# Batch loops written out, stack loads behind a stored-maxima wait, and VectorE taking ScalarE's copies at the end of the attention

## The reference

```python
mod = (silu(c) @ wmod).reshape(8, 6, 1, 128)          # sa, ca, ga, sb, cb, gb per batch
h = layernorm(x) * (1 + ca) + sa
q, k, v = split(h @ w_qkv)                            # 16 heads of 8
x = x + ga * (softmax(q k^T / sqrt(128)) v) @ w_out
h = layernorm(x) * (1 + cb) + sb
scores = softmax(h @ w_router)                        # top 2 of 8, renormalised
x = x + gb * sum_e comb[e] * ((silu(h w_gate[e]) * (h w_up[e])) @ w_down[e])
```

## Time and profile before

| what | value |
|---|---|
| device time, median of 3 runs | 664.18 us (663.45 to 664.81) |
| profiled execution, its own device time | 666.58 us |
| its span, first to last instruction | 664.8 us |
| mean granted TensorE clock | 0.96 |
| busy: PE, DVE, ACT, POOL | 609.4, 545.0, 443.4, 267.2 us |
| attention, first exponential of batch 1 to that of batch 2 | 49.30 us |

### The profile page before, as it was taken

One profiled execution on the slowest core, in us unless ns is written; L12 is line 12 of the kernel. 1 busy time (PEld: TensorE's weight loads), 2 busy tenths in 40 slices (PEclk: granted clock), 3 DMA queues, 4 the chain that ended last, 5 costly groups with the idle time before them and its releaser, 6 DMA issues.

```text
span 664.8 us, 12806 instructions
## 1 busy us (share of the span) xinstructions
PE 609.4 (92%) x3349; PEld 282.7 (43%) x3349; DVE 545.0 (82%) x1033; ACT 443.4 (67%) x843; POOL 267.2 (40%) x384
## 2 busy tenths in 40 slices
PE   4299999999999999999999999898899999999995
PEld 3112223322322322322322322226677777777773
DVE  3698889999998999998999999417788888888884
ACT  1207878878878778878778878875465555555552
POOL 4422012222222222222222212434576786786763
PEclk9757999999999999999999999979899999999997
DMA  7712604404304304304304301154244445344401
GB/s 187 178 56 61 210 4 97 131 19 97 131 20 97 129 18 97 130 19 97 129 18 97 130 19 47 50 156 142 80 129 157 129 136 149 126 142 142 133 26 32
DMA packets 49084, 65.58 MB, mean 99 GB/s; under 512 B 9544, under 2 KB 30544, under 8 KB 49040
## 3 DMA queue, kind: packets, MB, share of 16 engines
q1 hardware_dynamic: 46416, 64.32, 33.3%
q10 hardware_dynamic: 2624, 0.79, 0.5%
HBM read 47.26 MB, written 17.83 MB: 98 GB/s over the span
## 4 chain that ended last, share of the span: by engine, by line
PE 44%; issue 17%; POOL 16%; DVE 12%; ACT 6%; DMA 2%; SPq 1%; ACTq 1%; DVEq 1%; POOLq 0%
PE o_acc L1169 15%; POOL hid_lo L601 14%; PE s_row L1142 12%; PE s_col L1155 7%; DVE negmax L853 7%; ACT probs L645 4%; DVE probs L1032 2%; PE misc L1107 1%; POOL h_lo L607 1%; PE misc L1093 1%; PE misc L1090 1%; SPq L308 1%; PE misc L1123 1%; ACT oT L649 1%; PE misc L1119 1%
## 5 line engine op out<-in xcount | busy, mean ns | idle before, releaser
L853 DVE TENSOR_REDUCE negmax<-s_row 128x1 f32<-128x512 f32 x512 | 321.6, 682 | 37.9 <-PE s_row L1142 37.1
L645 ACT ACTIVATE probs<-s_col 128x512 f32<-128x512 f32 x512 | 273.6, 599 | 75.0 <-PE s_col L1155 72.0
L1142 PE MATMUL s_row<-k_stack,q_stack 64*128 64x512 bf16 x512 | 142.4, 403 | 23.8 <-DMA k_stack<-k_scr 11.0
L601 POOL TENSOR_TENSOR hid_lo<-probs,hid_hi 128x512 fp32r<-128x512 f32 x87 | 128.5, 1493 | 61.3 <-ACT hid_hi L789 61.3
L1169 PE MATMUL o_acc<-probs,v_aug 128*32 128x512 f32 x1024 | 138.1, 612 | 0.0
L1155 PE MATMUL s_col<-q_stack,k_stack 64*128 64x512 bf16 x512 | 132.3, 384 | 6.1 <-ACT probs L645 5.1
L789 ACT ACTIVATE hid_hi<-probs 128x512 fp32r<-128x512 f32 x88 | 55.6, 632 | 86.3 <-DVE probs L1032 86.0
L1142 PEld LDWEIGHTS s_row<-k_stack,q_stack 64*128 64x128 bf16 x512 | 36.0, 93 | 177.7 <-DVE negmax L853 138.5
L1032 DVE TENSOR_TENSOR probs<-probs,q_stack 128x512 f32<-128x512 f32 x56 | 62.3, 1112 | 15.6 <-POOL hid_lo L601 13.5
L509 POOL CAST negmax_parts<-negmax 128x16 bf16<-128x16 f32 x32 | 6.3, 196 | 166.9 <-DVE negmax L853 166.9
L1022 DVE TENSOR_TENSOR probs<-probs,s_col 128x512 f32<-128x512 f32 x88 | 59.6, 677 | 3.0 <-ACT probs L809 1.6
(11 more groups left out here) (134 smaller groups left out, 684.6 us busy)
## 6 DMA issues: line engine op xcount, KB each, us to landing
q_scr<-q_parts SPq DMA_DIRECT2D x48, 128.0 KB, 2.4
k_scr<-k_parts SPq DMA_DIRECT2D x48, 128.0 KB, 2.4
q_stack<-q_scr SPq DMA_DIRECT2D x8, 768.0 KB, 6.0
k_stack<-k_scr SPq DMA_DIRECT2D x8, 768.0 KB, 7.4
q_stack<-combT_scr SPq DMA_DIRECT2D x24, 256.0 KB, 3.3
k_stack<-combT_scr SPq DMA_DIRECT2D x16, 224.0 KB, 2.8
q_stack<-combT_scr SPq DMA_DIRECT2D x16, 192.0 KB, 2.8
q_stack<-combT_scr SPq DMA_DIRECT2D x16, 160.0 KB, 2.5
```

Of the source, the lines that this page charges most:

```text
L601: nc.gpsimd.tensor_tensor(hid_lo[k % HIDDEN][:], weighed[(par + k) % 2], hid_hi[k % HIDDEN][:], ALU.subtract).then_inc(s["hid_split"], 1)
L645: nc.scalar.activation(probs[t % 2][:, j, :], s_col[score_bank("col", u)][:], ACT.Exp, scale=INV_SCALE).then_inc(s["exp_done"], 1)
L853: nc.vector.tensor_reduce(negmax[n % 2][:, j, qc:qc + 1], s_row[score_bank("row", u)][:], AX.X, ALU.max, negate=True).then_inc(s["row_max" ...
L1142: nc.tensor.matmul(s_row[score_bank("row", u)][:], q_stack[par][at:at + KS, head // 2, P * qc:P * (qc + 1)], k_stack[par][at:at + KS, head ...
```

## The change

Three things. `over_batches` writes all 8 batches out on every engine in both phases, with no loop and the batch number a constant. `load_stacks` waits for one more semaphore: the stacks of batch b are loaded only when the stored maxima of group 2 of batch b-1 have landed. And in slots 8 to 15 of the last batch, VectorE does what ScalarE did there: the two `save_o`, the high part of the down weights (at the start of slot 11 in VectorE's list, where ScalarE had it at the end of the middle of slot 10), `h2T`, the first h, and `combT`.

```diff
--- before.py
+++ after.py
@@ -22,6 +22,7 @@
     NG = H // G
     SLOTS = NG * CH
     AHEAD = 8
+    DRAIN = SLOTS - AHEAD
     NEXT_BLOCK = 4
     BACK = 5
     LAG = 3
@@ -276,11 +277,8 @@
 
         def over_batches(eng, body):
 
-            body(0, 0, True, False)
-            with eng.Fori(0, (B - 2) // 2) as i:
-                body(2 * i + 1, 1, False, False)
-                body(2 * i + 2, 0, False, False)
-            body(B - 1, 1, False, True)
+            for b in range(B):
+                body(b, b % 2, b == 0, b == B - 1)
 
         def group(b, n):
 
@@ -312,6 +310,8 @@
                     sp.wait_ge(s["more_stored"], 16 * 4)
                 sp.wait_ge(s["q_stored"], 16 * STORES * (b + 1))
                 sp.wait_ge(s["k_stored"], 16 * STORES * (b + 1))
+                if not (isinstance(b, int) and b == 0):
+                    sp.wait_ge(s["max_stored"], 16 * (group(b - 1, 2) + 1))
                 for r0, r1, stacked in ((0, G // 2, "stacked_first"), (G // 2, PAIRS, "stacked")):
                     for stack_sb, scr in ((q_stack[par], q_scr), (k_stack[par], k_scr)):
                         sp.dma_start(stack_sb[:, r0:r1, :], scr.rearrange("a m r n -> (a m) r n")[:, r0:r1]).then_inc(s[stacked], 16)
@@ -732,10 +732,10 @@
                     store_max(0, int(name[3:]))
                     place_max(0, 0, int(name[3:]))
 
-            MIDDLE_Q, MIDDLE_K, ROUTER_EXP, FIRST_BLOCK = (2, 0), (3, 0), (12, 0), (14, 1)
+            MIDDLE_Q, MIDDLE_K, ROUTER_EXP = (2, 0), (3, 0), (12, 0)
             STORE_MAX = {(1, 0): 1, (5, 0): 2, (9, 0): 3, (13, 0): 0}
             PLACE_MAX = {(2, 0): 1, (6, 0): 2, (10, 0): 3, (14, 0): 0}
-            SPLIT_WEIGHTS = {(2, 1): 0, (6, 1): 1, (10, 1): 2}
+            SPLIT_WEIGHTS = {(2, 1): 0, (6, 1): 1}
 
             def body(b, par, first, last):
                 for t in range(SLOTS):
@@ -743,7 +743,7 @@
                         at = (t, half)
                         if at == (0, 0) and first:
                             act.wait_ge(s["v_const"], 2)
-                        if half == 0 and t % (SHARE * CH) == 1:
+                        if half == 0 and t % (SHARE * CH) == 1 and not (last and t >= DRAIN):
                             if t > 1:
                                 save_o(b, par, t // (SHARE * CH) - 1)
                             elif not first:
@@ -752,8 +752,6 @@
                             middle_part(b + 1, q_parts[:, Q_MID, :], q_rest, "q_rest_ready", "q_mid")
                         if at == MIDDLE_K and not last:
                             middle_part(b + 1, k_parts[:, K_MID, :], k_rest, "k_rest_ready", "k_mid")
-                        if at == FIRST_BLOCK and last:
-                            block_high(0, 0)
                         for table, step in ((STORE_MAX, store_max), (PLACE_MAX, place_max)):
                             n = table.get(at)
                             if n is None or (n == 0 and last):
@@ -771,13 +769,12 @@
                         if at == ROUTER_EXP and not first:
                             evacuate(None, b - 1, 1 - par, "router")
                         name = TASKS.get(at)
-                        if name in tasks(first, last) and name != "router":
+                        if name in tasks(first, last) and name != "router" and not (last and name in ("x1T", "combT")):
                             of = owner(b, name)
                             evacuate(misc_use(b, first, last, name), of, 1 - par if of is not b else par, name)
 
             over_batches(act, body)
             load_table(ACT.Silu)
-            save_o(B - 1, 1, NO - 1)
 
 
             def hid_high(b, par, k, wait_ring):
@@ -886,6 +883,28 @@
                     nc.vector.tensor_tensor(r_logit[:], logits, r_max[:].unsqueeze(2).to_broadcast([P, CH, E]),
                                             ALU.subtract).then_inc(s["r_logit_ready"], 1)
 
+            def drain_o(b, par, n):
+                dve.wait_ge(s["pv_done"], SLOTS * b + SHARE * CH * (n + 1))
+                nc.vector.tensor_copy(oT[par][:, n, :], o_acc[:]).then_inc(s["o_saved"], 1)
+
+            def drain_split_down():
+                dve.wait_ge(s["w_loaded"], 16 * 3)
+                nc.vector.tensor_copy(wd_hi[:].rearrange("p k c -> p (k c)"), w_raw[:]).then_inc(s["w_high"], 1)
+
+            def drain_first_block():
+                dve.wait_ge(s["h_loaded"], 16)
+                nc.vector.tensor_copy(h_hi[0][:], h_raw).then_inc(s["h_high"], 1)
+
+            def drain_task(use, b, name):
+
+                dve.wait_ge(s["misc_full"], use + 1)
+                if name == "x1T":
+                    dve.wait_ge(s["h2T_kept"], 16 * b)
+                    nc.vector.tensor_scalar(h2T[:], misc_f, mod[:, CB, b:b + 1], mod[:, SB, b:b + 1], ALU.mult, ALU.add).then_inc(s["h2T_ready"], 1)
+                elif name == "combT":
+                    dve.wait_ge(s["combT_kept"], 16 * b)
+                    nc.vector.tensor_copy(combT[:], misc_f[0:E, :]).then_inc(s["combT_ready"], 1)
+
             def ln2_stats(b, k):
 
                 if k == 0:
@@ -966,6 +985,7 @@
 
 
             REST = {(1, 2): "q", (2, 2): "k"}
+            SPLIT_DOWN, FIRST_BLOCK = (11, 0), (14, 1)
             LN2_STATS = {(6, 1): (0, 1), (7, 0): (2, 3), (7, 1): (4,)}
             ROUTE = {(12, 1): softmax_sum, (13, 0): sort, (13, 1): pick, (14, 0): denominator}
 
@@ -986,6 +1006,14 @@
                             if at in ROUTE:
                                 ROUTE[at](b - 1)
                         name = TASKS.get(at)
+                        if last and half == 0 and t >= DRAIN and t % (SHARE * CH) == 1:
+                            drain_o(b, par, t // (SHARE * CH) - 1)
+                        if last and at == SPLIT_DOWN:
+                            drain_split_down()
+                        if last and at == FIRST_BLOCK:
+                            drain_first_block()
+                        if last and name in ("x1T", "combT"):
+                            drain_task(misc_use(b, first, last, name), b - 1, name)
                         if name in tasks(first, last) and name not in REST.values():
                             of = owner(b, name)
                             evacuate(misc_use(b, first, last, name), of, 1 - par if of is not b else par, name)
@@ -1042,6 +1070,7 @@
                             denominator(B - 1)
                             pick(B - 1)
 
+            drain_o(B - 1, 1, NO - 1)
             over_batches(dve, block_body)
 
             dve.wait_ge(s["hid_high"], KT * B)
```

## The result

The change makes the kernel faster: 654.6 us median of 4 runs (654.47 to 655.25), against 664.0 for the kernel before beside it (4 runs, 663.45 to 664.81). The ratio is 0.985, with a 95% interval of 0.9821 to 0.988. The profiled execution took 654.47 us, its span is 652.8. The forecast was 657.2, with a range of 654.2 to 661.3. The direction was right and the parts were named rightly, but one of them was sized wrong: the register instructions stood in the sum with 0.15 us a batch, and gave 0.69.

The account below looks back on a forecast made before the run. In the attention no engine is full, three hand tiles round; in the experts VectorE and GpSimd alternate. 2.66 + 0.9 + 0.85 + 3.4 - 0.1 = 7.7 us, 666.58 to 658.9 profiled; median predicted 657.2, range 654.2 to 661.3.

Parts of the forecast that it names:

- register instructions: Attention: constants remove wait-count instructions in six batches; 0.15 us a batch, 0.9 in all, upper end 0.5 a batch, 3.0.
- The loop's jumps: Attention: two jumps back, which stall ScalarE and lengthen two batches, go; 2.66 us.
- The experts' boundaries: Experts: GpSimd's longer waits at five batch boundaries in looped code go; 0.17 us each, 0.85 together.
- The stack loads: Attention: loads issued later, behind the stored maxima, still come in time; no cost and no gain.
- The copies at the end: Last batch, slots 11 to 13: ScalarE freed of copies gives 1.15 us, the clock's dip the rest; 3.4 in all.
- The last copy: End of the attention: the last `save_o` takes 0.67 us on VectorE for ScalarE's 0.60; a loss of 0.1.
- Rival (d): Attention and its end: registers give their upper end and the clock's dip goes; 654.4 us, chance 0.08.
- Rival (a): Clock gives nothing, dip comes anyway at slot 10 or was absent unprofiled; registers give nothing; 659.6 us, chance 0.20.
- (b): Written-out batches: long straight code stalls in its turn and eats the gain; about 664 us, no change, chance 0.07.
- (c): Attention, slot 8 of seven batches: stack loads come late and row tiles wait; slower, 666 us, chance 0.05.
- Slot 10: Last batch: keeps its delay, its first exponential waiting 1.34 us for the store of the maxima; no gain.

Follow-up runs that it names:

- e5_act_loop: The kernel before with loops written out on all engines but ScalarE, which keeps the loop and its register instructions: 664.05 us.
- g2_registers: The whole change, straight code, but with the batch number of batches 2 to 6 in a register, so counts are computed again: 659.5 us.
- e4_stack: The kernel before with only the added wait of the stack loads for the stored maxima: 665.04 us, ratio 0.9993.
- e1_unroll: The kernel before with the batches written out, nothing else: 655.19 us, ratio 0.984.
- e3_experts: The kernel before with only the experts' phase written out, the attention still looped: 663.6 us, ratio 0.9985.
- f4_no_copies: The whole change without the copies on VectorE in the last batch: 656.68 us.
- f2: The whole change, with the load of the down weights waiting for the last store of maxima and their VectorE copy moved to slot 12: 655.04 us.
- g1: The whole change with gate weights split in batch 0, and up and down weights loaded and split earlier: 654.89 us.
- g3: The whole change with VectorE alone looped again, in the experts' stage only: 659.07 us.
- f3: The whole change once more, unaltered, beside f4_no_copies on the same chip: 654.57 us.
- g5: g1 with GpSimd's low part of the down weights moved behind the second normalisation in the last batch: 652.83 us, ratio 0.9829.
- e2_drain: The kernel before with only the copies of the end moved to VectorE, loops kept: 662.71 us, ratio 0.9953.
- f1_one_trip: The whole change, but each of batches 1 to 6 in a loop of one trip: 656.14 us, ratio 0.9872.

## Why the prediction was right or wrong

**The loop's jumps** (2.66 us): right. The two long batches were 1.25 and 1.32 over the ordinary ones, 2.57 together, and all of it is gone. ScalarE's jump alone gives it (e5_act_loop), as the chain in the earlier trace rows had it; TensorE's and VectorE's lengthen no batch. An expert with a branch behind it takes 24.63 in the kernel before, and 24.64 in g2_registers, which has none. So the stall that the Trainium skill (Runtime: NRT & Kernel Launch, Instruction fetch mechanics) has for a taken branch to code that is not held doesn't show in the experts. Whether their code was still held no run shows; the trace has 123 instructions of ScalarE from one jump to the next there, and 410 in the attention.

**The register instructions** ("I take 0.15 a batch, 0.9 in all"): this is the term that failed, in size only. It measured 0.69 a batch, 4.1 in all. I had bounded it by 3.0 and then taken the value near nothing, because the experts' low parts run alike in looped and written-out code. That was the wrong row to lean on. There GpSimd waits for the same engines in both, and the one place at which its register instruction came late I had read as the jump. In the attention three engines take turns, and each computes counts right behind a wait. Even the upper end, 0.5, was too low: it looked at the batch's start alone, while the loss is spread over six slots. That this term is the registers, and not the loop, is shown by g2_registers, straight code in which they bring back 49.28.

**The experts' boundaries** (0.85): right in size (0.9 in the last row of the table, less the last copy), wrong in cause. The rows at 511.82 and 536.51 stand in the middle of an expert. g2_registers, which has no branch, has such a wait of 1.37 in each of five experts, and its experts are as long (24.64 us); with the constants it is gone. The further 0.08 at 536.51 is not in g2_registers, but the expert with it is no longer than the others.

**The stack loads** (0): right. e4_stack has the ordinary batches of the kernel before to 0.02 us, and its long ones to 0.22.

**The copies at the end** (3.4, of it 1.15 for ScalarE's wait and the rest clock): right for the profiled execution, where slots 11 to 13 gave 3.8. Slot 11 went from 3.88 at full clock (e1_unroll) to 2.63, so 1.25 for 1.15. The clock's part is not a constant. Of eight profiles without the copies four have it at half from the end of slot 11 on (the kernel before for 6.8 us; e3_experts, e5_act_loop and f4_no_copies for 13.7 each), and four have not; of twelve with the copies none has it there. But a fall can also come one slot earlier, with the copies moved or not: in slot 10 the clock is at half for 3.4 us in four of the twelve (f2, g1, g2, g3) and in one of the eight (e4_stack), and that slot then takes 4.6 to 5.0 us instead of 3.3 to 3.8. So the copies give 1.25 in every profile, and the fall behind slot 11 in some. Between the medians of f3 and f4 that makes 2.1. I had left open whether the runs behind the median have the fall; the medians say that they have it in part.

**The last copy** (-0.1): 0.69 on VectorE for 0.60; too small to be seen in a time.

**The sum.** 7.7 was forecast for the profiled executions and 12.0 measured. 3.2 of the missing 4.3 are the registers, 0.6 the end, and 0.5 the time up to batch 1, which none of my steps touches: 0.3 of it lies in slot 1 of batch 0, which varies between 3.97 and 4.92 us over all profiles, whatever the kernel. With the registers at 4.1 the sum for the median would have been 10.9, or 8.5 without the clock's 2.4; measured were 9.4. Rival (d), "the registers give their upper end", came nearest with its 654.4, in part by luck: the registers gave 1.1 us more than its upper end, and the clock less than it had. Rival (a) has fallen as to the time; the dip at slot 10 that it named does come, in some profiles. (b) and (c) have fallen too: no row shows a stall of straight code over 1 us at a batch's start, or a late stack.

**Slot 10.** I wrote that it keeps its delay because of the store. It kept it, but the store was one of two waits that ended within 0.01 us of each other. f2 and g1 took the one away, and their medians gained nothing; in their profiles TensorE still waited 0.93 us for the normalised rows, and the clock fell in that slot besides. g5 shortened the other wait to 0.29 as well, and gained 1.2.

## What to carry to other kernels

Count the instructions that compute wait counts in a loop, and look for those that stand right behind a wait: where several engines hand tiles round, each of them is on the path, and 0.07 to 0.14 us in six of a batch's 16 slots is 1.4% of its 49 us. A row in which an engine stays busy says nothing on it; compare a looped and a written-out batch slot by slot. When a wait is taken away, look for the second one that ends at the same instant on another engine, as removing one alone can leave the slot as long as it was. And a part measured alone can read far from its share: e1_unroll by itself gave a ratio as good as the whole change's (0.984), e2_drain 0.9953, and both include the clock of the same few slots.

## What the runs showed of the hardware

- A product of 128x512 on VectorE beside GpSimd's subtraction of two SBUF operands: 0.69 us if it starts 0.11 us ahead, 1.79 if it starts 0.05 behind. Adding register instructions to one of two such engines costs more (4.85 us in g3_dve_experts) than adding them to both (0.17 us an expert).
- TensorE's clock at 0.50 in one stretch of the end for 0 (e1_unroll), 3.4 (e4_stack, in slot 10), 6.8 (before) or 13.7 us (e3_experts), in kernels that have the same code there. With the copies moved: none from slot 11 to 15 in twelve profiles, 3.4 us in slot 10 in four of them.
- A register instruction takes 0.03 to 0.05 us (g2_registers, before); 107 of them a batch on ScalarE lengthen it by 0.38 us.
- Two register instructions a batch and a branch that does not go back lengthen none of batches 1 to 6 (f1_one_trip).
